# DLRM tower on one Trainium2 core: each 128-row gather is issued only when the one before it has landed

## The chip, the core and the metric

The kernel runs on one NeuronCore of one Trainium2 chip. Five engines work from queues of their own and meet through semaphores: TensorE (PE) multiplies, VectorE (DVE) and ScalarE (ACT) work element by element, GpSimd (POOL) here only issues gathers, and SyncE (SP) issues the plain transfers. All transfers share 16 DMA engines. The metric is device time in microseconds of one execution, lower being better; it is given as the median of several runs.

## What is computed

A batch of 2048 samples has 32 table ids each. Every id picks a row of 64 fp32 numbers from one of 32 tables, and all 496 pairs of these rows are combined through a 64 x 64 matrix of their own. The results, with 16 dense numbers per sample, go through three small layers. The reference, cut to what matters:

```python
def _L0_rec_ref(x, kernel):                       # x: [2048, 32, 64]
    row_idx, col_idx = np.triu_indices(nf, k=1)
    p = x[:, row_idx, :]
    q = x[:, col_idx, :]
    kp = jnp.einsum('bpe,fpe,bpf->bp', p, kernel, q)
    return kp
e = jnp.stack([tbl_0[ids[:, 0]], tbl_1[ids[:, 1]], ...], axis=1)
z = _L0_rec_ref(e, L0_rec_kernel)
h = jnp.concatenate([z, dense_ctx], axis=1)
h = jnp.maximum(h @ W_top1 + b_top1, 0.0)
h = jnp.maximum(h @ W_top2 + b_top2, 0.0)
y = h @ W_top3
```

## The kernel before

**Tiling.** A gather fetches one table's rows for 128 samples: 128 rows of 256 bytes, 32 KB, one row per partition. There are 16 sample tiles and 32 tables, so 512 gathers. The samples are cut into four chunks of 512 and worked on in five segments `g`: chunk 0 as two segments of two tiles, chunks 1 to 3 as one segment of four tiles each. Two tables make a pair `q` (16 pairs); a pair takes 4 gathers in the first two segments and 8 in the last three.

**POOL.** After it has made a small identity matrix, POOL has nothing in its queue but the 512 gathers (line 375 before, 383 after), in the order segment, pair, table of the pair, tile. Pairs 0 to 3 go to `kept_rows` (two copies, by chunk parity); pairs 4 to 15 go to `rows`, a ring of four pairs (`ROW_RING`). So the gathers of pair q wait, once per pair, until PE has turned pair q-4 (semaphore `unit_ready`), and the kept pairs of chunks 2 and 3 wait for the last product of the chunk two before. Apart from these waits POOL issues one gather behind the other and never asks whether one has landed. Each gather adds 16 to the semaphore `landed(g, q)` of its pair's buffer when it has landed; it is PE that waits for these, in `turn`.

**PE, DVE and ACT.** A list `ORDER`, written out by hand through `BURSTS`, sets one order of 566 units for all engines. A "turn" unit transposes the gathered rows of one or two pairs (line 433) and DVE copies them to `xt` (line 743). "duo" and "quad" units multiply transposed pairs with their matrices on PE (lines 475 to 491), and DVE multiplies the result with another pair (lines 712, 720). "batch" units do the same against the kept pairs (PE lines 497 and 499, DVE line 731), and ACT (or DVE for some) sums their products (line 637). PE then adds up the products over partitions (line 511) and computes the layers (lines 527, 530; the last chunk's in `last_tower`, lines 544 to 559). PE's results go through a ring of three PSUM buffers `y_ps`, ACT's sums through a ring of four. A turn of pair q comes at the place that `ORDER` gives it, and everything behind it on PE waits with it.

**SP.** At the start SP loads the ids, the pair matrices (7.75 MB) and the weights; later it copies small pieces between `xt` and `special`, and writes the outputs.

Of the kernel before, what the change touches and what calls it, by code (L numbers as in the profile page):

```python
# [17 lines left out]
SEGMENTS = ((0, 0, 2), (0, 2, 4), (1, 0, 4), (2, 0, 4), (3, 0, 4))  # L18
PAIRS = F // 2

KEPT = 4
ROW_RING = 4
# [21 lines left out]
def chunk(g):  # L44
    return SEGMENTS[g][0]


def tiles(g):

    return range(SEGMENTS[g][1], SEGMENTS[g][2])  # L50
# [10 lines left out]
def first_of(c):  # L61
    return min(g for g in range(len(SEGMENTS)) if chunk(g) == c)
# [17 lines left out]
def duo_order():  # L80

    duos = []
    for q in range(1, PAIRS):
# [5 lines left out]
        elif q == PAIRS - 1:  # L89
# [14 lines left out]
LAYERS = ([(1, n, kb) for n in range(4) for kb in range(4)] + [(2, n, kb) for n in range(2) for kb in range(4)]  # L104
          + [(3, 0, kb) for kb in range(2)])
GROUPS = 7
BANK_ENDS = [min(QUADS, Z_QUADS * (kb + 1)) - 1 for kb in range(Z_BANKS)]


# [70 lines left out]
TURN_OF = {(unit[1], q): g for g, unit in enumerate(UNIT) if unit[0] == "turn" for q in unit[2]}  # L180
# [44 lines left out]
def dlrm_tower(nc, ids, tables, pair_kernel, dense, w1, b1, w2, b2, w3, out):  # L225
    with ExitStack() as ctx:
# [3 lines left out]
        def sem(name):  # L230
            return ctx.enter_context(nc.semaphore(name))
# [41 lines left out]
        unit_ready = sem("unit_ready")  # L273
# [15 lines left out]
        def rows_of(g, q, t):  # L289
            if q < KEPT:  # L290
                return kept_rows[:, chunk(g) % 2, t, 2 * q:2 * q + 2]
            return rows[:, (q - KEPT) % ROW_RING, t]

        def lane(g):

            return int(SEGMENTS[g][1] > 0)

        def landed(g, q):
            return kept_landed[lane(g)][q] if q < KEPT else rows_landed[lane(g)][(q - KEPT) % ROW_RING]

        def landings(g, q):

            uses, own = (1, 1) if q < KEPT else ((PAIRS - KEPT) // ROW_RING, (q - KEPT) // ROW_RING + 1)
            before = sum(len(tiles(i)) for i in range(g) if lane(i) == lane(g))
            return 2 * 16 * (uses * before + own * len(tiles(g)))

        def z_of(c, kb):
            return z_sb[:, (c * Z_BANKS + kb) % Z_RING] if kb < Z_BANKS else z_turned[:]

# [37 lines left out]
        def group(c, layer, n):  # L347
            return c * GROUPS + {1: n, 2: 4 + n, 3: 6}[layer]

        block = ctx.enter_context(nc.Block())  # L350

        @block.gpsimd
        def _(pool):
            nc.gpsimd.memset(identity[:], 0.0).then_inc(identity_cleared, 1)
            pool.wait_ge(identity_cleared, 1)
            nc.gpsimd.affine_select(out=identity[:], in_=identity[:], compare_op=ALU.not_equal, fill=1.0, base=0,
                                    pattern=[[-1, P]], channel_multiplier=1).then_inc(identity_made, 1)
            for g in range(len(SEGMENTS)):
                c, before = chunk(g), first_of(chunk(g)) - 1
                if g == 0:  # L360
                    pool.wait_ge(ids_landed[0], 16)
                elif g == first_of(1):
                    pool.wait_ge(ids_landed[1], 16)
                for q in range(PAIRS):
                    if q < KEPT and c >= 2:
                        pool.wait_ge(unit_done, max(UNIT_OF[unit] for unit in BATCH if chunk(unit[1]) == c - 2) + 1)
                    elif q >= KEPT + ROW_RING:
                        pool.wait_ge(unit_ready, TURN_OF[g, q - ROW_RING] + 1)
                    elif q >= KEPT and c:
                        pool.wait_ge(unit_ready, TURN_OF[before, q - ROW_RING + PAIRS - KEPT] + 1)  # L370
                    for h in range(2):
                        j = 2 * q + h
                        for t in tiles(g):
                            n = c * TILES + t
                            pool.indirect_dma_start(rows_of(g, q, t)[:, h, :], None, tables[j],  # L375
                                                    bass.IndirectOffsetOnAxis(ap=idx[:, n, j:j + 1], axis=0)
                                                    ).then_inc(landed(g, q), 16)
# [50 lines left out]
        def _(pe):  # L428
# [74 lines left out]
            def add_up(g, quad):  # L503
# [5 lines left out]
                for m in range(4):  # L509
                    slot, place = product_of(g, 2 * quad + m // 2)  # L510
                    last = nc.tensor.matmul(sum_ps[32 * m:32 * m + 32, columns(g)], selector[:, 30 - 2 * s:62 - 2 * s],  # L511
                                            products[:, slot, m % 2, place],
                                            start=(s == 0 and not last_bank), stop=(quad in BANK_ENDS))
                last.then_inc(quad_summed, 1)
# [90 lines left out]
        def _(act):  # L605
# [3 lines left out]
            def copy_bank(g, kb):  # L609
                act.wait_ge(quad_summed, SUM_OF[g, BANK_ENDS[kb]] + 1)  # L610
                c = chunk(g)
                if c and kb == 1:
                    act.wait_ge(layer_ready, group(c - 1, 1, 3) + 1)
                copy(z_of(c, kb)[:, columns(g)], sum_ps[:, columns(g)]).then_inc(bank_kept, 1)
# [28 lines left out]
            for step in ORDER:  # L643
                kind = step[0]
                if kind == "sum" and step[2] in BANK_ENDS:
                    copy_bank(step[1], step[2] // Z_QUADS)
# [147 lines left out]
```

## Time and profile before

| | us |
|---|---|
| median of 3 runs | 1267.82 |
| lowest and highest run | 1261.34 to 1269.45 |
| span of the profiled execution | 1281.0 |
| of which PE busy / DVE busy / ACT busy | 845.6 / 656.8 / 685.0 |
| POOL busy (512 gathers and a few small instructions) | 484.9 |

The profiled execution is 13 us (1.0%) above the median. An engine is "busy" while it executes; a POOL row for a gather covers only the making of the transfer's descriptors, not the transfer. The transfer itself shows as packets on the DMA queue called software_dynamic: 16384 of them in all, so 32 for each gather: 16 of 2 KB with the rows and 16 of 4 bytes that raise the semaphore.

### The profile page before, as it was taken

To read this page: it belongs to the slowest core of one execution; us is meant where nothing else is said; L and a number is where in the kernel's file an instruction comes from. 1 tells how busy PE (TensorE), PEld (TensorE's weight loads), DVE (VectorE), ACT (ScalarE), POOL (GpSimd) and SP (SyncE) were. 2 spreads that over 40 slices of the span, in tenths; PEclk is the share of its full clock that TensorE was granted. 3 is DMA by queue.
4 is the path that set the end of the run, shared out by engine and by line. 5 is a ranking of instruction groups with operands and counts; after the bars stand their busy time and mean duration, and the time that the engine had idled before them with its cause. 6 is when DMAs were issued, how large, how long until landed. Compare 5 with 4: busy or idle time off the path is not lost.

```text
span 1281.0 us, 16495 instructions
## 1 busy us (share of the span) xinstructions
PE 845.6 (66%) x4672; PEld 330.6 (26%) x4672; DVE 656.8 (51%) x601; ACT 685.0 (53%) x5196; POOL 484.9 (38%) x518
## 2 busy tenths in 40 slices
PE   0570596603589658526899566028898856889999
PEld 0230253301344212102233122002233312223333
DVE  0350495401467445215689355016697545768881
ACT  0281295713255643106698525226696645779991
POOL 7557204575302454762400643755402244220000
PEclk9785697856789778757889777558899888889999
DMA  9111001111001110110101110210000101010000
GB/s 335 30 38 26 10 10 26 28 27 28 15 13 25 34 19 17 41 25 9 33 2 20 24 32 14 43 19 17 18 17 9 27 17 34 9 26 2 1 18 1
DMA packets 34644, 36.40 MB, mean 28 GB/s; under 512 B 18676, under 2 KB 20980, under 8 KB 34424
## 3 DMA queue, kind: packets, MB, share of 16 engines
q0 software_dynamic: 16384, 16.81, 7.1%
q1 hardware_dynamic: 18168, 18.53, 5.1%
q8 instruction: 37, 0.61, 0.2%
q14 instruction: 55, 0.45, 0.1%
HBM read 26.91 MB, written 0.01 MB: 21 GB/s over the span
## 4 chain that ended last, share of the span: by engine, by line
PE 45%; another core or an unknown queue 29%; issue 12%; DVE 11%; POOL 1%; DMA 1%; ACT 0%; DVEq 0%
PE y_ps L475 12%; PE y_ps L497 10%; PE sum_ps L511 8%; DVE batch_products L731 4%; DVE products L720 4%; PE layer_ps L527 4%; PE y_ps L490 3%; PE layer_ps L530 2%; DVE products L712 2%; PE y_ps L433 2%; POOL kept_rows L375 1%; PE y_ps L478 1%; PE y_ps L544 1%; PE y_ps L491 1%
## 5 line engine op out<-in xcount | busy, mean ns | idle before, releaser
L637 ACT ACTIVATE batch_products<-batch_products 128x64 f32<-128x64 f32 x2576 | 618.5, 243 | 298.8 <-issue 170.5
L375 POOL DMA_INDIRECT rows<-tbl_dram,idx x384 | 363.1, 945 | 613.3 <-PE y_ps L433 490.1
L637 ACT ACTIVATION_READ_ACCUMULATOR batch_products<-batch_products 128x1 f32 x2576 | 488.4, 190 | 123.2 <-issue 122.0
L720 DVE TENSOR_TENSOR products<-y_ps,xt 128x1024 f32<-128x1024 f32 (+1 forms) x224 | 258.5, 1200 | 260.8 <-remote 194.2
L475 PE MATMUL y_ps<-xt,kernel_sb 64*128 64x512 f32 (+1 forms) x448 | 233.3, 649 | 137.5 <-issue 78.5
L731 DVE TENSOR_TENSOR batch_products<-y_ps,kept_rows 128x1024 f32<-128x1024 f32 x192 | 225.5, 1217 | 92.7 <-remote 56.1
L497 PE MATMUL y_ps<-kernel_sb,xt 64*128 64x512 f32 x384 | 214.0, 683 | 71.7 <-DVE products L720 24.6
L476 PE MATMUL y_ps<-xt,kernel_sb 64*128 64x512 f32 (+1 forms) x448 | 233.4, 649 | 0.0
L499 PE MATMUL y_ps<-kernel_sb,xt 64*128 64x512 f32 x384 | 213.8, 683 | 0.0
L511 PE MATMUL sum_ps<-products,selector 128*32 128x512 f32 (+1 forms) x1520 | 162.4, 543 | 26.3 <-issue 10.9
L712 DVE TENSOR_TENSOR products<-y_ps,xt 128x1024 f32<-128x1024 f32 x68 | 79.8, 1218 | 160.5 <-remote 95.2
L475 PEld LDWEIGHTS y_ps<-xt,kernel_sb 64*128 64x128 f32 x448 | 80.5, 197 | 279.4 <-issue 172.2
L490 PE MATMUL y_ps<-xt,kernel_sb 64*128 64x256 f32 x272 | 83.0, 447 | 84.9 <-issue 46.5
L375 POOL DMA_INDIRECT kept_rows<-tbl_dram,idx x128 | 121.2, 947 | 40.3 <-issue 38.7
L497 PEld LDWEIGHTS y_ps<-kernel_sb,xt 64*128 64x128 f32 x384 | 72.2, 210 | 168.7 <-issue 60.6
L491 PE MATMUL y_ps<-xt,kernel_sb 64*128 64x256 f32 x272 | 83.7, 449 | 9.8 <-issue 9.8
L490 PEld LDWEIGHTS y_ps<-xt,kernel_sb 64*128 64x128 f32 x272 | 56.2, 217 | 106.4 <-issue 54.4
L476 PEld LDWEIGHTS y_ps<-xt,kernel_sb 64*128 64x128 f32 x448 | 80.4, 197 | 0.0
L511 PEld LDWEIGHTS sum_ps<-products,selector 128*32 128x32 f32 x1520 | 42.3, 114 | 136.6 <-issue 71.4
L743 DVE COPY xt<-y_ps 128x512 f32<-128x512 f32 (+2 forms) x58 | 42.6, 738 | 65.3 <-PE y_ps L433 43.2
L499 PEld LDWEIGHTS y_ps<-kernel_sb,xt 64*128 64x128 f32 x384 | 72.2, 210 | 0.2
L491 PEld LDWEIGHTS y_ps<-xt,kernel_sb 64*128 64x128 f32 x272 | 56.5, 218 | 14.0 <-issue 13.6
(54 smaller groups left out, 415.2 us busy)
## 6 DMA issues: line engine op xcount, KB each, us to landing
kernel_sb<-pair_kernel_dram SPq DMA_DIRECT2D x15, 512.0 KB, 4.9
rows<-tbl_dram,idx POOLq DMA_INDIRECT x384
special<-xt SPq DMA_DIRECT2D x48, 128.0 KB
kept_rows<-tbl_dram,idx POOLq DMA_INDIRECT x128
special<-xt SPq DMA_DIRECT2D x32, 64.0 KB
w_sb<-w_dram SPq DMA_DIRECT2D x1, 1024.0 KB
w_sb<-w_dram SPq DMA_DIRECT2D x1, 512.0 KB
kernel_sb<-pair_kernel_dram SPq DMA_DIRECT2D x1, 256.0 KB, 2.7
```

The costliest lines, as they stand in the source:

```text
L375: pool.indirect_dma_start(rows_of(g, q, t)[:, h, :], None, tables[j], bass.IndirectOffsetOnAxis(ap=idx[:, n, j:j + 1], axis=0)).then_inc(l ...
L475: nc.tensor.matmul(y[:, 0, :], kernel_sb[low, d, :], x_of(g, q)[low, :], start=True, stop=True)
L476: last = nc.tensor.matmul(y[:, 1, :], kernel_sb[high, d, :], x_of(g, q)[high, :], start=True, stop=True)
L490: nc.tensor.matmul(y[:, 0, place], kernel_sb[low, d, :], x_of(g, q)[low, :], start=True, stop=True)
L491: last = nc.tensor.matmul(y[:, 1, place], kernel_sb[high, d, :], x_of(g, q)[high, :], start=True, stop=True)
L497: nc.tensor.matmul(y[:, 0, :], x[low, :], kernel_sb[low, d:d + KEPT, :].rearrange("p d f -> p (d f)"), start=True, stop=True)
L499: nc.tensor.matmul(y[:, 1, :], x[high, :], kernel_sb[high, d:d + KEPT, :].rearrange("p d f -> p (d f)"), start=True, stop=True).then_inc(u ...
L511: last = nc.tensor.matmul(sum_ps[32 * m:32 * m + 32, columns(g)], selector[:, 30 - 2 * s:62 - 2 * s], products[:, slot, m % 2, place], sta ...
L637: last = nc.scalar.activation(product, product, ACT.Copy, accum_out=batch_sums(unit)[:, column:column + 1])
L712: nc.vector.tensor_tensor(into.rearrange("p b (d n) -> p b d n", d=2), y[:].rearrange("p b (d n) -> p b d n", d=2), by, ALU.mult).then_inc ...
L720: nc.vector.tensor_tensor(into[:, :, 0:size], y[:, :, 0:size], by, ALU.mult).then_inc(unit_done, 1)
L731: nc.vector.tensor_tensor(into, y[:], by, ALU.mult).then_inc(unit_done, 1)
```

## The change

One wait is put in front of every gather but the first. `FLIGHT` lists the 512 gathers in the order of issue; before a gather is issued, POOL waits until the semaphore of the gather issued last has reached the count that it has when exactly that gather has landed (`landed_by`).

```diff
+FLIGHT = [(g, q, h, t) for g in range(len(SEGMENTS)) for q in range(PAIRS) for h in range(2) for t in tiles(g)]
...
+        def landed_by(g, q, h, t):
+
+            return landings(g, q) - 16 * ((1 - h) * len(tiles(g)) + tiles(g)[-1] - t)
...
-                c, before = chunk(g), first_of(chunk(g)) - 1
+                c, last = chunk(g), first_of(chunk(g)) - 1
...
-                        pool.wait_ge(unit_ready, TURN_OF[before, q - ROW_RING + PAIRS - KEPT] + 1)
+                        pool.wait_ge(unit_ready, TURN_OF[last, q - ROW_RING + PAIRS - KEPT] + 1)
                     for h in range(2):
                         j = 2 * q + h
                         for t in tiles(g):
                             n = c * TILES + t
+                            if FLIGHT.index((g, q, h, t)):
+                                before = FLIGHT[FLIGHT.index((g, q, h, t)) - 1]
+                                pool.wait_ge(landed(*before[:2]), landed_by(*before))
                             pool.indirect_dma_start(rows_of(g, q, t)[:, h, :], None, tables[j],
```

`FLIGHT` and `before` are evaluated when the program is built; on the chip only the waits are new. The renaming of `before` to `last` changes nothing. No instruction of another engine is added, removed or moved.

POOL's queue at the start of the first segment, before the change, with the semaphores that each gather waits for:

```order
L375 DMA kept_rows<-tbl_dram,idx 128x64 [waits ids_landed0]
L375 DMA kept_rows<-tbl_dram,idx 128x64 x15
L375 DMA rows<-tbl_dram,idx 128x64 x16
L375 DMA rows<-tbl_dram,idx 128x64 [waits unit_ready]
L375 DMA rows<-tbl_dram,idx 128x64 x3
```

The same place after the change, where `kept_landed` and `rows_landed` are the semaphores that the gathers themselves raise:

```order
L383 DMA kept_rows<-tbl_dram,idx 128x64 [waits ids_landed0]
L383 DMA kept_rows<-tbl_dram,idx 128x64 [waits kept_landed0_0] x4
L383 DMA kept_rows<-tbl_dram,idx 128x64 [waits kept_landed0_1] x4
L383 DMA kept_rows<-tbl_dram,idx 128x64 [waits kept_landed0_2] x4
L383 DMA kept_rows<-tbl_dram,idx 128x64 [waits kept_landed0_3] x3
L383 DMA rows<-tbl_dram,idx 128x64 [waits kept_landed0_3]
L383 DMA rows<-tbl_dram,idx 128x64 [waits rows_landed0_0] x4
L383 DMA rows<-tbl_dram,idx 128x64 [waits rows_landed0_1] x4
L383 DMA rows<-tbl_dram,idx 128x64 [waits rows_landed0_2] x4
L383 DMA rows<-tbl_dram,idx 128x64 [waits rows_landed0_3] x3
L383 DMA rows<-tbl_dram,idx 128x64 [waits rows_landed0_3,unit_ready]
```

Before, 31 gathers in a row stood behind the first with no wait at all. Now each one waits for its predecessor, and the waits for the ring stay where they were.

## Rows read from the trace of the kernel before

**Rows 1.** The page: busy time, tenths over 40 slices, shares of the chain.
```profile
PE 845.6 (66%) x4672; PEld 330.6 (26%) x4672; DVE 656.8 (51%) x601; ACT 685.0 (53%) x5196; POOL 484.9 (38%) x518
...
DVE  0350495401467445215689355016697545768881
...
POOL 7557204575302454762400643755402244220000
PEclk9785697856789778757889777558899888889999
...
PE 45%; another core or an unknown queue 29%; issue 12%; DVE 11%; POOL 1%; DMA 1%; ACT 0%; DVEq 0%
```
**Rows 2.** The chain that ended last, 85 to 300 us: start, us, what.
```profile
92.61 41.02 issue
...
246.39 39.95 another core or an unknown queue
```
**Rows 3.** Windows inside long rows of gathers: bounds, length, busy us (instructions) per engine.
```profile
core 0: us, PE busy (x) PEld busy (x) DVE busy (x) ACT busy (x) POOL busy (x), PEclk, DMA share, GB/s
92.60:133.60 41.00, 3.17 (x14) 1.15 (x10) 0.01 (x1) 8.86 (x46) 31.18 (x33) 0.57 0.15 27
247.00:292.00 45.00, 3.85 (x32) 2.35 (x28) 1.23 (x2) 10.80 (x56) 34.00 (x36) 0.56 0.15 27
800.00:854.00 54.00, 6.58 (x24) 2.02 (x20) 2.45 (x2) 11.11 (x53) 40.89 (x44) 0.55 0.18 36
```
**Rows 4.** Windows with (almost) no gather, same columns.
```profile
640.00:702.60 62.60, 59.25 (x328) 21.52 (x330) 55.38 (x49) 58.59 (x478) 0.03 (x1) 0.95 0.06 11
1139.50:1253.00 113.50, 111.40 (x558) 39.70 (x560) 95.39 (x85) 103.07 (x828) 0.00 (x0) 0.97 0.03 6
```
**Rows 5.** The first 5 us of a row of 40 gathers, same columns.
```profile
87.60:92.60 5.00, 5.00 (x46) 2.52 (x48) 5.00 (x5) 5.00 (x44) 3.78 (x5) 1.00 0.26 68
```
**Rows 6.** POOL's gathers by line: xcount, busy us, mean ns, idle before them.
```profile
L375 POOL DMA_INDIRECT rows<-tbl_dram,idx x384 | 363.1, 945 | 613.3 <-PE y_ps L433 490.1 <-issue 105.8 <-remote 15.8
L375 POOL DMA_INDIRECT kept_rows<-tbl_dram,idx x128 | 121.2, 947 | 40.3 <-issue 38.7 <-DMA idx<-ids_dram 1.6
```
**Rows 7.** Timeline around four gathers: start, us, engine, idle before and releaser.
```profile
3.02 1.10 POOL L375 DMA_INDIRECT kept_rows<-tbl_dram,idx  x1 [1.55 <-DMA idx<-ids_dram]
...
81.45 0.95 POOL L375 DMA_INDIRECT rows<-tbl_dram,idx  x1 [0.30 <-issue]
82.70 0.95 POOL L375 DMA_INDIRECT rows<-tbl_dram,idx  x1 [0.30 <-issue]
...
86.92 0.41 PE L433 MATMUL y_ps<-identity,rows 64*128 64x64 f32 x8
87.60 0.94 POOL L375 DMA_INDIRECT rows<-tbl_dram,idx  x1 [3.95 <-PE y_ps L433]
```
**Rows 8.** DMA packets from 82.69 us, first up to 84.79, then up to 84.85.
```profile
DMA packets 64, 0.07 MB, mean 35 GB/s; under 512 B 31, under 2 KB 31, under 8 KB 63
...
DMA packets 65, 0.07 MB, mean 34 GB/s; under 512 B 32, under 2 KB 32, under 8 KB 64
```
**Rows 9.** DMA packets from 0.70 us, first up to 2.39, then up to 2.45.
```profile
DMA packets 151, 0.08 MB, mean 49 GB/s; under 512 B 15, under 2 KB 143, under 8 KB 151
...
DMA packets 155, 0.09 MB, mean 50 GB/s; under 512 B 16, under 2 KB 144, under 8 KB 155
```
**Rows 10.** A gather's way under load (chain, 0 to 60 us); DMA queues, 0 to 33 us.
```profile
26.95 5.76 DMA rows<-tbl_dram,idx
...
q1 hardware_dynamic: 5397, 10.05, 86.8%
```
**Rows 11.** The last turns of the program on PE: start, us, engine line.
```profile
1155.55 0.46 PE L433 MATMUL y_ps<-identity,rows 64*128 64x64 f32 x8
...
1192.10 0.46 PE L433 MATMUL y_ps<-identity,rows 64*128 64x64 f32 x8
...
1221.16 0.46 PE L433 MATMUL y_ps<-identity,rows 64*128 64x64 f32 x8
```

## The prediction, made before the changed kernel was run

> **What bounds the kernel now.** I read the page first. No engine is busy for more than 66% of the 1281.0 us, and 41% of the chain that ended last is work of nobody: 29% "another core or an unknown queue" and 12% "issue" [rows 1]. The line of DVE over 40 slices is low where that of POOL is high, and the granted TensorE clock falls there too. Then I read the longest pieces of that chain: 41.02 us from 92.61 and 39.95 us from 246.39 [rows 2]. Windows laid over them show what they are. Each lies inside a long row of gathers issued back to back (40, 40 and 48 gathers around the three windows). In 41 us of the first, DVE does nothing, PE executes 14 matmuls and ACT 46 instructions, while POOL goes on with 33 gathers [rows 3]. In windows without gathers the same program keeps PE busy for 98% of 113.5 us and 95% of 62.6 us, DVE for 84% and 88% [rows 4]. The first five microseconds of a row of gathers are not slow: PE, DVE and ACT are busy all the time in 87.60:92.60 [rows 5], and the standstill begins right behind them. So the kernel has two kinds of time: without gathers, where PE and DVE are nearly full, and long rows of gathers, where everybody but POOL all but stands still. POOL itself is no bound: of its idle time before the `rows` gathers 490.1 us of 613.3 is a wait for PE's turns [rows 6].
>
> How much is lost: DVE's 656.8 us busy at 84 to 88% would take 750 to 780 us. The other 500 of 1281.0 are start-up (33 us) and time beside gathers. The change could give much of that back, since it spaces the gathers. What it costs is POOL's own pace.
>
> **The change part by part.** Nothing is removed or moved. 511 waits are added on POOL, and behind a waiting gather stand only further gathers; PE's turns wait for those, and DVE and ACT for PE. The ring waits stay. What counts is the period, from the start of one gather to the start of the next.
>
> Before, it is 1.25 us: 82.70 less 81.45 [rows 7], that is 0.95 execution and 0.30 to the next. After, it is the way of one gather to its semaphore plus POOL's reaction.
>
> - The way: between 82.69 and 87.60 fall the packets of two gathers, that of 82.70 and the one before it, with 32 packets under 512 B. Up to 84.79, 31 of them have run, up to 84.85 all 32 [rows 8]. So the last four-byte packet runs 2.1 to 2.15 us after the start: 2.12.
> - The reaction: the trace has no gather that waits for another. The nearest row is POOL's wait for the ids: their 16th small packet has run by 2.42 (between 2.39 and 2.45) [rows 9], and POOL starts at 3.02 [rows 7], 0.60 later. The lower bound is the reaction to an engine's semaphore: PE's turn ends at 87.33 and POOL starts at 87.60 [rows 7], 0.27. I take 0.58, near the first, since that also is a semaphore raised by DMA packets.
>
> The period is then 2.70 us, with 2.39 and 2.75 as bounds. At the start it is longer: while SP's loads keep the DMA engines 87% busy, a gather took 5.76 us to land [rows 10]; with 0.27 that makes 6.0. From 3.0 to 33 us that is 5 gathers. The other 507 at 2.70 take 1369 us, so the last gather lands at about 1402 us. That alone is more than the span of 1281.0. In the old kernel POOL needed 512 x 1.25 = 640 us and waited for the rest.
>
> Does POOL also wait for the ring in between? A pair of 8 gathers takes 21.6 us, and POOL runs up to four pairs ahead. Without standstills PE needs about 780 us for what amounts to 64 such pairs, 12 us each. So PE waits for POOL and the ring is empty; I put POOL's ring waits at 0. The gain from no standstills is hidden in these waits of PE: it makes PE faster between turns, where it then waits anyway.
>
> The tail: PE turned pair 13 of the last segment at 1155.55, pair 14 at 1192.10, pair 15 at 1221.16, and ended at 1281.0 [rows 11]. From turn 13 to the end is 125.5 us, at nearly full speed with no gathers beside it [rows 4]. The steps between, 36.6 and 29.1, are both longer than 21.6, so once pair 13 has landed PE is behind and works through. Pair 13 lands 16 gathers before the last: 1402 - 16 x 2.70 = 1359. The end is 1359 + 125.5 = 1484 us. In a formula: 33 + (507 - 16) x period + 125.5. The measured median lies 13 us below the profiled span, so 1471; I say 1470, 16% slower.
>
> Two rules of the Trainium skill bear on this. DMA: Bandwidth & Descriptors, section "Anatomy of one DMA — SWDGE (gpsimd) path", gives a gather of this kind about 2.0 us plus bytes over 436 GB/s, an estimate of 2.08 us for 32 KB; the trace's 2.12 to the last packet agrees. If that figure held all the way to the semaphore, with 0.27 for the reaction, the period would be 2.35 and the end 33 + 491 x 2.35 + 125.5 = 1312, so 1299; that falls into the second rival below. Trainium Architecture — The Big Picture, section "What this means for kernel authors", says that the engines are independent processors and that one does not block another unless a semaphore stands between them. By that rule gathers could not hold up DVE, and spacing them would give nothing back. What slows DVE in a row of gathers would then be something else and could remain, which is the first rival's time. The trace speaks against the rule here: in 41 us with 33 gathers DVE did 0.01 us of work [rows 3].
>
> **The rivals.**
> - *The standstill stays.* Each gather costs the other engines a fixed time, however far apart the gathers are. In the three windows DVE is busy for 3.7 of 140 us, 3% [rows 3] against 84%, so it loses 1.2 of each 1.25 us; with the free start of a row [rows 5] I take 1.1. At a period of 2.70 they would then run at 1 - 1.1/2.70 = 60% of full speed, and 780 us of work would take 1300, close to POOL's 1369, so PE would fall behind where `ORDER` has much work between turns. The two steps of the tail, 65.6 us, would take up to 109, and PE would come to turn 13 some 30 us late: 1484 + 43 + 30 = 1557, so about 1545. For it: only that the mechanism isn't known. Against it: five gathers in [rows 5] cost nothing at all, so what fails fails through a build-up, and at 2.70 us there is more than twice the time to drain it.
> - *The reaction is short.* With 0.27 the period is 2.39, the end 33 + 491 x 2.39 + 125.5 = 1332, so 1319. For it: the PE row. Against it: the ids row.
> - *Not slower.* The standstills go, and a gather that runs alone lands sooner than one with a neighbour. It decides where 33 + 491 x period + 125.5 is 1281, at a period of 2.28 us. The packets alone take 2.12, so only 0.16 would be left for the semaphore and POOL, less than the smallest reaction seen, 0.27. And packets of neighbours don't overlap now: 81.45 and 82.70 are 1.25 apart. To be faster by 1% the period would have to be 2.25.
> - *PE at the lower clock.* PE will wait often, and in windows where it waits much the granted clock is 0.55 to 0.57 of full speed [rows 3], which is mostly the 1.2 GHz level, against 0.95 and 0.97 where it works [rows 4]. Between turns there is slack for this; in the tail it may cost 10 to 40 us. That gives up to 1510.
>
> **How the numbers follow.** The forecast (period 2.6 to 2.75, other engines nearly free, 1430 to 1500) gets 0.65; the lower clock or some leftover standstill with 1500 to 1560 gets 0.2; a short reaction with 1310 to 1430 gets 0.11; not slower gets 0.04. The range is 1395 to 1550: it leaves out a little of both ends. A measurement of this kernel can tell about 1% from no change. Slower by over 1%: 0.96; within 1%: 0.02; faster: 0.02.
>
> **What would show it.** POOL's gathers should start 2.7 us apart almost without exception from 33 us on, with "DMA" as releaser, and its wait for PE's turns (490.1 us now) should be close to nothing. The last gather should start near 1400 us. PE should wait for DMA in front of nearly every turn, and the pieces of 40 us of "issue" and "unknown queue" should be gone. If DVE's busy share between turns stays low while PE has landed rows to turn, the first rival holds. The prediction is wrong if gathers come less than 2.4 us apart, or if POOL waits for turns again.

## The result and the profile after

| | kernel before | changed kernel |
|---|---|---|
| median, us | 1267.3 (4 runs, 1261.34 to 1269.45) | 1536.18 (4 runs, 1531.42 to 1538.41) |
| profiled execution: time / span | span 1281.0 | 1536.28 / 1534.5 |
| mean granted TensorE clock, share of full speed | 0.813 | 0.779 |

The change makes the kernel 21% slower: the ratio is 1.212, with a 95% interval of 1.208 to 1.216. 1470 was forecast, with a range of 1395 to 1550. The time lies in the range, 66 us above the forecast.

The page of the changed kernel, first the busy times, then the tenths over 40 slices, last the shares of the chain that ended last (these answer to [rows 1]):

```profile
PE 838.8 (55%) x4672; PEld 342.6 (22%) x4672; DVE 659.8 (43%) x601; ACT 646.7 (42%) x5196; POOL 483.5 (32%) x518
...
DVE  0033740435514324326474203543572435664882
...
PEclk9986975768757767779697556876896777897999
...
DMA 74%; PE 15%; issue 10%; DVE 1%; DVEq 0%; ACT 0%; POOLq 0%
```

The work is the same, but the chain is another. "Another core or an unknown queue" was 29% of it and is gone. 74% of the chain is now "DMA": one gather behind the other on its way to its semaphore.

POOL's gathers by line, with the idle time before them and its releasers (answers to [rows 6]), and then PE's two longest waits (total us, times, longest):

```profile
L383 POOL DMA_INDIRECT rows<-tbl_dram,idx x384 | 362.0, 943 | 716.5 <-DMA rows<-tbl_dram,idx 658.9 <-PE y_ps L441 40.0 <-DMA kept_rows<-tbl_dram,idx 5.6
L383 POOL DMA_INDIRECT kept_rows<-tbl_dram,idx x128 | 120.8, 944 | 248.7 <-DMA kept_rows<-tbl_dram,idx 228.0 <-DMA rows<-tbl_dram,idx 8.5 <-issue 5.9
```
```profile
PE y_ps L441 <- DMA rows<-tbl_dram,idx: 500.3, 50, 22.8
PE y_ps L441 <- DMA kept_rows<-tbl_dram,idx: 187.0, 15, 26.7
```

POOL now waits for landings, 658.9 + 5.6 + 228.0 + 8.5 = 901 us in all, where it had waited 490.1 us for PE's turns. PE waits for rows 65 times, 687 us in all.

The timeline of POOL at three places: start, us, then in brackets the idle time before it and what ended it.

```profile
31.17 0.94 POOL L383 DMA_INDIRECT kept_rows<-tbl_dram,idx  x1 [3.41 <-DMA kept_rows<-tbl_dram,idx]
...
101.36 0.94 POOL L383 DMA_INDIRECT rows<-tbl_dram,idx  x1 [1.74 <-DMA rows<-tbl_dram,idx]
104.54 0.94 POOL L383 DMA_INDIRECT rows<-tbl_dram,idx  x1 [2.24 <-PE y_ps L441]
107.21 0.94 POOL L383 DMA_INDIRECT rows<-tbl_dram,idx  x1 [1.73 <-DMA rows<-tbl_dram,idx]
...
1445.69 0.94 POOL L383 DMA_INDIRECT rows<-tbl_dram,idx  x1 [1.75 <-DMA rows<-tbl_dram,idx]
1448.44 0.94 POOL L383 DMA_INDIRECT rows<-tbl_dram,idx  x1 [1.81 <-DMA rows<-tbl_dram,idx]
```

The step from 104.54 to 107.21 is 2.67 us and that from 1445.69 to 1448.44 is 2.75; over the whole trace the median step is 2.70. But the step from 101.36 to 104.54 is 3.18 us. The gather at 104.54 is the first of a pair, so it has the wait for the ring in front of its landing wait. The last gather starts at 1448.4.

Two windows of the changed kernel near its end, one with gathers and one without (columns as in [rows 3]):

```profile
core 0: us, PE busy (x) PEld busy (x) DVE busy (x) ACT busy (x) POOL busy (x), PEclk, DMA share, GB/s
...
1410.00:1448.00 38.00, 38.00 (x176) 13.62 (x174) 29.85 (x27) 34.70 (x281) 12.87 (x14) 0.98 0.07 13
1450.00:1505.00 55.00, 54.94 (x292) 19.66 (x286) 46.19 (x41) 51.25 (x414) 0.00 (x0) 1.00 0.05 11
```

With 14 gathers in 38 us, PE is busy all of the time and DVE for 79% of it, against 84% in the window with none. At this pace gathers hardly disturb anybody. In the rows of the kernel before DVE was busy for 0.01 us of 41 [rows 3].

The last turns on PE (start, us, what; they answer to [rows 11]):

```profile
1406.37 0.69 PE L441 MATMUL y_ps<-identity,rows 64*128 64x64 f32 x8 [10.67 <-DMA rows<-tbl_dram,idx]
...
1445.54 0.46 PE L441 MATMUL y_ps<-identity,rows 64*128 64x64 f32 x8
...
1474.61 0.46 PE L441 MATMUL y_ps<-identity,rows 64*128 64x64 f32 x8
```

Pair 13 is the last for which PE waits, 10.67 us. Behind it PE works through: 39.2 us to the next turn, 29.1 to the one after, 59.9 to the end.

### The profile page after: what moved, and what is told of

It reads as the page before. It is cut to its first block, busy times and chain, and to the rows that moved or that the text cites. A ratio compares the mean times of both kernels' runs of the same rounds, so it can differ in the third digit from the quotient of the medians.

```text
span 1534.5 us, 16556 instructions
## 1 busy us (share of the span) xinstructions
PE 838.8 (55%) x4672; PEld 342.6 (22%) x4672; DVE 659.8 (43%) x601; ACT 646.7 (42%) x5196; POOL 483.5 (32%) x518
## 4 chain that ended last, share of the span: by engine, by line
DMA 74%; PE 15%; issue 10%; DVE 1%; DVEq 0%; ACT 0%; POOLq 0%
DMA rows<-tbl_dram,idx 55%; DMA kept_rows<-tbl_dram,idx 19%; PE y_ps L505 4%; PE y_ps L483 4%; PE sum_ps L519 3%; PE y_ps L441 1%; PE layer_ps L535 1%; PE layer_ps L538 1%; PE y_ps L552 1%; PE y_ps L498 1%; PE y_ps L561 0%; DVE products L728 0%; PE y_ps L556 0%; DMA idx<-ids_dram 0%; PE y_ps L486 0%
## 5 line engine op out<-in xcount | busy, mean ns | idle before, releaser
L383 POOL DMA_INDIRECT rows<-tbl_dram,idx x384 | 362.0, 943 | 716.5 <-DMA rows<-tbl_dram,idx 658.9
L441 PE MATMUL y_ps<-identity,rows 64*128 64x64 f32 x384 | 33.0, 300 | 500.6 <-DMA rows<-tbl_dram,idx 500.3
L505 PE MATMUL y_ps<-kernel_sb,xt 64*128 64x512 f32 x384 | 245.0, 780 | 1.7 <-DVE xt L751 1.5
L507 PE MATMUL y_ps<-kernel_sb,xt 64*128 64x512 f32 x384 | 244.8, 780 | 0.0
L483 PE MATMUL y_ps<-xt,kernel_sb 64*128 64x512 f32 (+1 forms) x448 | 208.9, 601 | 0.3 <-DVE products L728 0.3
L484 PE MATMUL y_ps<-xt,kernel_sb 64*128 64x512 f32 (+1 forms) x448 | 208.9, 601 | 0.0
L383 POOL DMA_INDIRECT kept_rows<-tbl_dram,idx x128 | 120.8, 944 | 248.7 <-DMA kept_rows<-tbl_dram,idx 228.0
L519 PE MATMUL sum_ps<-products,selector 128*32 128x512 f32 (+1 forms) x1520 | 172.2, 571 | 3.1 <-DVE products L720 1.4
L441 PEld LDWEIGHTS y_ps<-identity,rows 64*128 64x128 f32 x384 | 23.9, 189 | 533.9 <-issue 288.2
L441 PE MATMUL y_ps<-identity,kept_rows 64*128 64x64 f32 x128 | 11.0, 302 | 187.4 <-DMA kept_rows<-tbl_dram,idx 187.0
L505 PEld LDWEIGHTS y_ps<-kernel_sb,xt 64*128 64x128 f32 x384 | 88.3, 249 | 104.5 <-issue 61.2
L483 PEld LDWEIGHTS y_ps<-xt,kernel_sb 64*128 64x128 f32 x448 | 78.8, 188 | 134.0 <-issue 81.0
L507 PEld LDWEIGHTS y_ps<-kernel_sb,xt 64*128 64x128 f32 x384 | 88.3, 249 | 0.0
L484 PEld LDWEIGHTS y_ps<-xt,kernel_sb 64*128 64x128 f32 x448 | 78.8, 188 | 0.0
L498 PE MATMUL y_ps<-xt,kernel_sb 64*128 64x256 f32 x272 | 71.2, 410 | 0.3 <-DVE products L720 0.3
```

The costliest lines, as they stand in the source:

```text
L441: return nc.tensor.transpose(into, rows_of_tile[part, :], identity[part, part])
L483: nc.tensor.matmul(y[:, 0, :], kernel_sb[low, d, :], x_of(g, q)[low, :], start=True, stop=True)
L484: last = nc.tensor.matmul(y[:, 1, :], kernel_sb[high, d, :], x_of(g, q)[high, :], start=True, stop=True)
L498: nc.tensor.matmul(y[:, 0, place], kernel_sb[low, d, :], x_of(g, q)[low, :], start=True, stop=True)
L505: nc.tensor.matmul(y[:, 0, :], x[low, :], kernel_sb[low, d:d + KEPT, :].rearrange("p d f -> p (d f)"), start=True, stop=True)
L507: nc.tensor.matmul(y[:, 1, :], x[high, :], kernel_sb[high, d:d + KEPT, :].rearrange("p d f -> p (d f)"), start=True, stop=True).then_inc(u ...
```

## The experiments

Two questions were open. Where do the 66 us over the forecast come from? And what is the standstill beside rows of gathers, which the change removes at so high a price? The runs were made in four groups, each with the kernel before beside it, and the groups differ in a way that nothing in the profile of before had announced:

| runs | kernel before beside them, us |
|---|---|
| chip A: every 2nd, every 4th, every 8th, extra wait | 1266.95 |
| chip B: every 6th, spacer, few sums, plain transfers | 794.48 (13 runs, 794.44 to 795.12) |
| chip C: changed kernel again, spacer again | 794.43 (7 runs) |
| chip D: ring wait last, a repeat of the kernel before | 1287.12 (13 runs, 1279.88 to 1291.69) |

The same program takes 1267 to 1287 us on two chips and 794 us on two others. Which chip the main result came from isn't on record; its two times, 1267.3 and 1536.18 us, are those of chip A (1266.95, and 1536.48 with the extra wait), and it is counted with A below. Each ratio is against the kernel before on the same chip.

### Fewer landing waits: every 2nd, 4th, 8th gather (chip A)

In the changed kernel only every 2nd gather waits for the one ahead of it; in two more kernels the 2 is a 4 and an 8. Between waiting gathers POOL issues back to back.

```diff
-                            if FLIGHT.index((g, q, h, t)):
+                            if FLIGHT.index((g, q, h, t)) and FLIGHT.index((g, q, h, t)) % 2 == 0:
```

Expected of every 2nd:

> POOL waits only ahead of every second gather, until the gather issued last has landed; the other is issued straight behind its neighbour. Two gathers then take 1.25 + 2.8 us, a mean pace of 2.0 us. Theory A (the standstill of the other engines builds up over a row of back-to-back gathers and drains in a gap; spaced gathers cost the others nothing): POOL's pace sets the end, 33 + 491 x 2.0 + 125.5 = 1140 us, and no piece of standstill is left. Rival B (each gather costs the others a fixed 0.9 us wherever it stands: before, 1281 less 33 less 780 is 468 us over 512 gathers): the others need 33 + 780 + 468 = 1281 whatever POOL does, so about 1280 us.

Expected of every 4th:

> The wait stands ahead of every fourth gather: three at 1.25 us and one at 2.8, a mean pace of 1.64 us. Theory A with a build-up that takes more than four gathers and drains in one gap: PE becomes the bound in the heavy stretches, POOL in the others, 33 + 491 x 1.64 + 125.5 = 965 us, up to 1050. If the gap of 1.5 us behind four gathers doesn't drain what they build up, standstills come back and the time lies above that of the kernel with every second. Rival B: about 1280 us.

Expected of every 8th:

> The wait stands ahead of every eighth gather: a mean pace of 1.44 us. Before, the others worked for about five gathers of a long row and then stood. Theory A: standstills return in the last gathers of each eight and in long rows carry over, so 1100 to 1250 us, slower than every fourth; if the gap drains everything, 870 to 1000. Rival B: about 1280 us.

Measured: every 2nd 1167.56 us (ratio 0.921, 0.917 to 0.925), every 4th 990.98 us (0.782, 0.779 to 0.785), every 8th 1106.45 us (0.874, 0.870 to 0.878). All three are faster than the kernel before on this chip, and the one in the middle is the fastest. The chain's shares, every 2nd first, then every 4th and every 8th:

```profile
DMA 44%; PE 26%; POOL 16%; issue 12%; DVE 2%; DVEq 0%; ACT 0%; POOLq 0%
```
```profile
PE 48%; POOL 21%; DMA 19%; issue 10%; DVE 2%; DVEq 0%; ACT 0%; POOLq 0%
```
```profile
PE 49%; another core or an unknown queue 14%; issue 13%; DVE 12%; ACT 8%; POOL 2%; DMA 2%; DVEq 0%
```

At every 2nd the chain is still the gathers' own way (DMA and POOL, 60%). At every 4th PE is the largest part and nothing of the standstill is left: DVE has two waits of 1.9 us in all that the trace puts down to an unknown queue, where in the kernel before there are 50 of 374.5 us. At every 8th the "unknown queue" is back with 14%. A window of every 4th in which most of the time goes to gathers, then one of every 8th:

```profile
core 0: us, PE busy (x) PEld busy (x) DVE busy (x) ACT busy (x) POOL busy (x), PEclk, DMA share, GB/s
242.00:283.00 41.00, 26.48 (x252) 14.88 (x252) 26.33 (x24) 20.32 (x168) 23.73 (x26) 0.91 0.13 27
```
```profile
core 0: us, PE busy (x) PEld busy (x) DVE busy (x) ACT busy (x) POOL busy (x), PEclk, DMA share, GB/s
246.30:261.60 15.30, 5.61 (x28) 2.96 (x24) 0.00 (x0) 7.05 (x51) 9.45 (x11) 0.68 0.13 24
```

With 26 gathers in 41 us DVE is busy for 26.33 us; with 11 in 15.3 us it does nothing. The timeline of every 8th shows how the standstill comes and goes, DVE's rows first, then POOL's:

```profile
244.98 1.23 DVE L739 TENSOR_TENSOR batch_products<-y_ps,kept_rows 128x1024 f32<-128x1024 f32 x1 [0.48 <-issue]
261.70 1.23 DVE L720 TENSOR_TENSOR products<-y_ps,xt 128x1024 f32<-128x1024 f32 x1 [15.50 <-remote]
```
```profile
240.00 0.95 POOL L383 DMA_INDIRECT kept_rows<-tbl_dram,idx  x1 [0.48 <-issue]
...
247.51 0.94 POOL L383 DMA_INDIRECT kept_rows<-tbl_dram,idx  x1 [0.30 <-issue]
250.17 0.94 POOL L383 DMA_INDIRECT kept_rows<-tbl_dram,idx  x1 [1.72 <-DMA kept_rows<-tbl_dram,idx]
...
261.56 0.95 POOL L383 DMA_INDIRECT kept_rows<-tbl_dram,idx  x1 [1.69 <-DMA kept_rows<-tbl_dram,idx]
```

DVE stops at 246.2, when six gathers of a group have been issued. A pause of POOL of 1.72 us at 250.17 does not set it free; it starts again only at 261.70, right behind the next one. So the price of the standstill is not so much per gather. It needs a build-up of more than four gathers, as [rows 5] had suggested, and once there it can outlast one pause. The build-up view forecast every 4th and every 8th rightly (965 to 1050, and 1100 to 1250) and every 2nd 28 us too low, with a mean pace of 2.0 us where 2.09 was measured; "each gather costs a fixed time" (1280 for every 2nd) was wrong by 112 us.

### An extra wait behind the landing wait (chip A)

Is the missing time a price per semaphore wait? POOL gets one more wait in front of every gather but the first, for a semaphore that was raised long ago.

```diff
                                 pool.wait_ge(landed(*before[:2]), landed_by(*before))
+                                pool.wait_ge(identity_cleared, 1)
```

> The changed kernel with one more wait ahead of each gather but the first, on a semaphore that has been up since the start. In the changed kernel POOL starts 0.58 us after a gather's last packet where it has one wait, and 1.05 us where the ring's wait stands there too, in 60 of 512 places. Theory C (a second wait instruction costs POOL 0.47 us though it is met): 511 x 0.47 = 240 us more, about 1775 us. Rival (the 0.47 us is a property of these places, such as a turn that was only just done): about 1535 us.

Measured: 1536.48 us (2 runs), beside the changed kernel's 1536.18. A met wait that stands behind the landing wait costs nothing; 511 of them change the time by 0.3 us. The price per wait is ruled out for this place. Ahead of the landing wait it is another matter, as the next run shows.

### The ring wait behind the landing wait (chip D)

In 60 places a gather of the changed kernel waits first for the ring (or for the last product of the chunk two before) and then for the landing. Here the two waits change places.

```diff
                     for h in range(2):
                         j = 2 * q + h
                         for t in tiles(g):
                             n = c * TILES + t
                             if FLIGHT.index((g, q, h, t)):
                                 before = FLIGHT[FLIGHT.index((g, q, h, t)) - 1]
                                 pool.wait_ge(landed(*before[:2]), landed_by(*before))
+                            if (h, t) == (0, tiles(g)[0]) and q < KEPT and c >= 2:
+                                pool.wait_ge(unit_done, max(UNIT_OF[unit] for unit in BATCH if chunk(unit[1]) == c - 2) + 1)
+                            elif (h, t) == (0, tiles(g)[0]) and q >= KEPT + ROW_RING:
+                                pool.wait_ge(unit_ready, TURN_OF[g, q - ROW_RING] + 1)
...
```

> The changed kernel with the two waits of a pair's first gather in the other order: first the landing of the gather before, then the ring's turn of PE (or the last product), in 60 places. In the changed kernel these gathers start 1.05 us after the last packet of the one before, all others 0.58; a met extra wait behind the landing wait cost nothing. Theory D (a landing wait costs 0.47 us more when another wait stands ahead of it): these too start after 0.58, the last gather starts 28 us earlier, the end is 1536 less 28, about 1508 us. Rival (the ring's wait itself is slow, in either order): about 1535 us.

Measured: 1513.76 us (1506.95 to 1518.03), ratio 1.174 (1.168 to 1.180) to the 1287.12 of chip D. The changed kernel itself did not run on chip D, so the comparison of times is across chips; the rows carry the argument. This is the gather that started 3.18 us behind its predecessor in the changed kernel:

```profile
101.73 0.94 POOL L383 DMA_INDIRECT rows<-tbl_dram,idx  x1 [1.81 <-DMA rows<-tbl_dram,idx]
104.42 0.94 POOL L383 DMA_INDIRECT rows<-tbl_dram,idx  x1 [1.74 <-DMA rows<-tbl_dram,idx]
...
1429.28 0.94 POOL L383 DMA_INDIRECT rows<-tbl_dram,idx  x1 [1.82 <-DMA rows<-tbl_dram,idx]
```

It now takes 2.69 us. Over all 60 such gathers the time from the last packet of the one ahead to the start is 0.56 us at the median, where it was 1.05 in the changed kernel and 0.58 for all other gathers. So 60 x 0.47 = 28 us of the changed kernel's time was the order of two waits. The last gather starts at 1429.3, only 19 us sooner, and the time is 1514 where 1508 was expected: in this run the ways were longer (2.141 us at the mean against 2.125, 8 us over 506 steps), as were the other landing waits (0.626 against 0.619, 3 us). One more place agrees. The first gather of chunk 1 has the wait for the second half of the ids, long met, ahead of its landing wait in both kernels, and it starts 1.09 and 1.04 us after the last packet. It isn't a wait for PE: in the changed kernel PE was itself waiting for rows. The releaser that the profile names for these gathers, PE's line 441 (40.0 us in 18 waits), is only the semaphore that stood first.

### Does the changed kernel know of the standstill? (chip C)

No edit; the changed kernel runs where the kernel before takes 794 us.

> The changed kernel as it is, once more. In the last four runs the kernel before took 794.5 us beside them, not 1267: no stretch in which all engines but GpSimd stand. Those four kernels therefore say what gathers cost without a standstill. Where the kernel before takes 1267 us here, this one should take 1536 again. Where it takes 794, theory P (the end is GpSimd's chain of gathers, and standstills play no part in it) gives 33 + 491 x 2.70 + 125.5 = 1484 us, up to 1536 if the late reactions of 1.05 us are there as well; the ratio to before would be 1.87 to 1.93 instead of 1.21. The rival (the changed kernel too lost time to standstills, 50 us or more) gives below 1440.

Measured: 1534.81 us (1532.74 to 1538.73), ratio 1.933 (1.930 to 1.937), with a span of 1531.4, the last gather at 1447.0 and a clock of 0.782. On chip A it took 1536.18. The changed kernel has the same time in both places; all the difference lies in the kernel before. The change costs 269 us in one and 740 in the other, and what could be worked out is the absolute time.

### Every 6th gather (chip B)

The 4 above is a 6.

```diff
-                            if FLIGHT.index((g, q, h, t)):
+                            if FLIGHT.index((g, q, h, t)) and FLIGHT.index((g, q, h, t)) % 6 == 0:
```

> The wait ahead of every sixth gather; mean pace 5 x 1.25 + 2.8, over 6, is 1.51 us. Measured so far: every gather 1536, every second 1168, every fourth 991, every eighth 1106 us, never 1267. Theory A: about five gathers are free and then the others stand, so six are near the turning point: 985 to 1050 us, above every fourth by what one or two gathers of standstill in each six cost (85 groups of about 1 us: 1030). If the pace alone counted (no standstill at six) it would be 960 to 980.

Measured: 912.12 us, ratio 1.148 (1.146 to 1.150) to the 794.48 there. It lies below both expectations, also below the 960 to 980 given for pace alone; that figure was too high by the prediction's own formula, which gives 900 us for a pace of 1.51 and 915 for the measured 1.54. Whether six gathers start a standstill can't be told from this run, since the kernel before shows no lost time on this chip. What it gives is one more point on how the end follows POOL's pace, taken up in the next section.

### A fixed pace without any landing wait (chips B and C)

The kernel before gets one small memset on POOL between gathers, and the next gather but one waits for it, so that gathers start farther apart, whether they have landed or not. It was to tell a standstill by rate from one by gathers in flight.

```diff
+                            i = FLIGHT.index((g, q, h, t))
+                            if i > 1:
+                                pool.wait_ge(paced, i - 1)
+                            if i:
+                                nc.gpsimd.memset(pace[:], 0.0).then_inc(paced, 1)
                             pool.indirect_dma_start(rows_of(g, q, t)[:, h, :], None, tables[j],
```

> The kernel before with no wait for a landing, but with one small memset on GpSimd between each gather and the next (its result is used by nobody), which should space the gathers evenly by 1.5 to 1.9 us. A gather takes 2.1 us to its last packet, so the next is always begun before the last has landed: the pipe never runs empty. Theory R (what counts is the rate of gathers; at this pace nothing builds up): no standstill, and the end near 33 + 491 x pace + 125.5, so 935 at 1.65, 1010 at 1.8. Theory L (what counts is that gathers land before the next is issued, an empty pipe now and then): long standstills remain, 1150 us or more.

> The kernel with a small memset between gathers and no wait for a landing, once more; it spaced the gathers by 1.39 us and took 849 us where the kernel before took 794. Where the kernel before takes 794 here: 849 again. Where it takes 1267, theory L (only an empty pipe now and then ends a build-up) gives a time near 1267 or above, 1150 to 1350; theory R (the rate counts) gives clearly less, 900 to 1100, since the rate is 11% lower at 1.39 us.

Measured: 848.86 us on chip B (ratio 1.068, 1.066 to 1.070) and 848.02 on chip C (1.068, 1.066 to 1.069). The gathers start 1.39 us apart, less than the 1.5 to 1.9 expected, and the chain's shares on chip B are:

```profile
POOL 55%; PE 36%; issue 8%; DMA 1%; DVEq 0%; POOLq 0%; DVE 0%; ACT 0%
```

So 0.14 us more per gather makes POOL the bound of a kernel in which, at 1.25, PE was nearly full (93% in the kernel with few sums below, where the last gather starts at 657.4, 56 us sooner, and the end comes 55 us sooner). Rate against in flight stays undecided: neither chip has a standstill to remove. A third kernel was meant for chip D, with three memsets per gather, but the one that ran held the tile and the semaphore for them and none of the memsets:

```diff
+        pace = sb("pace", [P, 192])
...
+        paced = sem("paced")
```

> No wait for a landing; three small memsets, each waiting for the one before, stand between gathers, in place of one. With one the pace was 1.39 us. Three should make it 2.1 to 2.4. Theory P (the end follows GpSimd's pace, whatever makes it): 3 + 495 x pace + 2.4 + 125.5, the start-up now without landing waits, so 1170 at 2.1 and 1320 at 2.4. Rival (waits for landing cost the other engines something beyond the pace): below this formula by more than 20 us. Where the kernel before takes 1267 us and not 794, theory L of the spacer kernel would put this one above the formula, with standstills; theory R on it.

Measured: 1285.57 us against 1287.12, ratio 0.999 (0.996 to 1.001). That is the kernel before once more, and nothing about pace follows from it. Its chain has the same kind of piece at the same place as [rows 2]:

```profile
92.54 46.55 another core or an unknown queue
```

### Three quarters of ACT's sums left out (chip B)

In the kernel before, ACT sums the products of every fourth column only; the rest of that result is zero. The question was whether the many small instructions of ACT make the standstill.

```diff
+                if column % 4 < 3:
+                    return
...
-            nc.vector.memset(z_batch[:, :, 0, :], 0.0).then_inc(z_cleared, 1)
+            nc.vector.memset(z_batch[:], 0.0).then_inc(z_cleared, 1)
```

> The kernel before (no waits for landing) in which ScalarE sums only every fourth of its columns, so the output lacks these sums; ScalarE issues 3864 instructions fewer of 16495. ScalarE was not the bound. Theory S (gathers and the instructions of all engines draw on one shared thing, so fewer instructions of ScalarE leave more for PE and DVE): the standstills begin later and the time falls well below 1267, to 1100 to 1200. Rival (a row of gathers stops each engine by itself): 1240 to 1270 us.

Measured: 794.38 us against 794.48, ratio 1.000 (0.999 to 1.001). ACT's busy time falls from 685.0 to 195.0 us and the time doesn't move, so ACT is far from the bound; on the standstill the run is silent. Its profile shows long rows of gathers at full pace on a chip without standstills. The page's busy times, and two windows:

```profile
PE 739.7 (93%) x4672; PEld 302.6 (38%) x4672; DVE 650.1 (82%) x601; ACT 195.0 (25%) x1332; POOL 484.1 (61%) x518
```
```profile
core 0: us, PE busy (x) PEld busy (x) DVE busy (x) ACT busy (x) POOL busy (x), PEclk, DMA share, GB/s
200.00:241.00 41.00, 37.05 (x283) 17.84 (x280) 33.34 (x30) 7.89 (x55) 30.94 (x34) 1.00 0.22 41
300.00:341.00 41.00, 41.00 (x226) 14.73 (x224) 36.96 (x35) 14.10 (x102) 30.94 (x34) 1.00 0.19 40
```

34 gathers in 41 us, as dense as in [rows 3] (33 in 41), and DVE is busy for 33 and 37 us, PE for 37 and 41. This kernel has fewer instructions of ACT than the kernel before, but on this chip their times are equal.

### Plain transfers in place of gathers (chip B)

The kernel before, with each gather replaced by a plain transfer from POOL's queue of the same shape, which always fetches a table's first 128 rows, so the results are of the wrong rows.

```diff
-                            pool.indirect_dma_start(rows_of(g, q, t)[:, h, :], None, tables[j],
-                                                    bass.IndirectOffsetOnAxis(ap=idx[:, n, j:j + 1], axis=0)
-                                                    ).then_inc(landed(g, q), 16)
+                            pool.dma_start(rows_of(g, q, t)[:, h, :], tables[j][0:P, :]).then_inc(landed(g, q), 16)
```

> The kernel before with each indirect gather replaced by a plain transfer of the first 128 rows of the same table, issued from GpSimd as before (so the rows are the wrong ones): same bytes, same destinations, same queue, same semaphores, no waits for landing. If the standstill comes from GpSimd-made transfers as such, long rows of them stop the engines again and the time is near 1267 where the pace is the same (1.0 to 1.3 us each). If it comes from the indirect form, there are no standstills and the time is 850 to 950 us.

Measured: 783.16 us (2 runs), ratio 0.986 (0.984 to 0.988). POOL's busy time is 270.3 us in place of 484.9, so 0.53 us for a transfer in place of 0.95. Being rid of the indirect form is worth 11 us on a chip without standstills. Whether plain transfers would cause one elsewhere is open.

## Why the prediction was right, and where its 66 us went

**How the end follows POOL.** In the runs in which the gathers' own pace sets the time, the end is the start of the last gather plus a tail, as the forecast had it.

| | mean pace, us | last gather starts | span | tail |
|---|---|---|---|---|
| changed kernel | 2.80 | 1448.4 | 1534.5 | 86 |
| ring wait last | 2.76 | 1429.3 | 1516.2 | 87 |
| every 2nd | 2.09 | 1071.3 | 1168.1 | 97 |
| every 4th | 1.71 | 878.6 | 993.9 | 115 |
| every 6th | 1.54 | 791.4 | 911.8 | 120 |
| spacer, chip B | 1.39 | 713.8 | 847.8 | 134 |

The forecast's tail was 1484 less the start of the last gather, about 1399: 85 us. Measured 86. It grows at faster paces, presumably because PE then has more left to do when the last gather lands. Every 8th is not in the table: there POOL waits for PE's turns again (227.5 us; mean pace 1.87, last gather at 960.1, tail 143), and the pace doesn't set the end.

Step by step:

- *The period, 2.70 us (2.12 way + 0.58 reaction).* Right as the median of the steps, to the hundredth. The ids row, not the PE row, was the one to go by. Single landing waits took 0.58 us at the median from the last packet to the start.
- *507 gathers at this period.* **The step that failed.** A typical step was taken for the mean. The mean from 31.17 to 1448.44 is 2.80 us (506 steps); 0.10 x 506 is 51 us, and the last gather starts 49 us later than forecast. 28 us of it are the 60 gathers that stand behind two waits (0.47 each), shown by the exchange of the waits. The rest, about 20 us, are single landing waits of more than 0.58 (their mean is 0.62, which makes 18 us over 446) and ways of more than 2.12 (mean 2.125, some 3 us); why these vary is open.
- *POOL's ring waits put at 0.* In the sense meant, right: PE was ahead, and no ring was ever full. But the wait instruction itself wasn't free where it stood, and the trace books 40.0 us under PE's name, most of which is the gather's own way running at the same time. The forecast priced the event and not the place of the wait.
- *The start-up, 5 gathers by 33 us.* Right: the gather behind the first five starts at 31.17. But its steps were 6.9, 5.5, 5.5, 5.8 and 4.3 us where 6.0 was taken for each, so the agreement of the sum is in part luck.
- *The tail from turn 13.* 128.1 us against 125.5, its steps 39.2 and 29.1 against 36.6 and 29.1. Pair 13 was turned at 1406.4, 47 us after the 1359 forecast; this is the mean period again.
- *Minus 13 us for the median.* Wrong. The 13 us between the median and the span of before belonged to one execution of the kernel before and not to the profile as such. It may have been how long its standstills lasted, or another chip (on chip D its spans are 1278 to 1290 us); the record doesn't tell. The changed kernel's profiled execution took 1536.28 us, 1.8 above its span and level with its median. This step cost 13 + 2 us.

Summed: 47 (pair 13 late) + 3 (tail) + 13 + 2 = 65, and the miss is 66 us.

**The rivals.** *The standstill stays* named a time, 1545, that lies nearer to the result than the forecast, but its mechanism is refuted: with 14 gathers in 38 us PE is full, DVE is busy for 79%, and the two steps of the tail take 68.3 us together, where this rival had up to 109. *The short reaction* (2.39) and *not slower* (2.28; its equation gives 2.29) fall with the period. *PE at the lower clock*: in the window 1410 to 1448 the granted clock is 0.98, mostly the 2.4 GHz level, and 1.00 behind it, as PE waits for nothing there. In the slack it was low: the clock of 0.779 over the whole span shows it. It cost at most the 2.6 us by which the tail is longer.

The Trainium skill, DMA: Bandwidth & Descriptors, section "Anatomy of one DMA — SWDGE (gpsimd) path", gives about 2.0 us plus bytes over 436 GB/s, an estimate of 2.08 us here. By itself it is close to the 2.12 us to the last packet, but a kernel that chains gathers pays 2.70 per gather, and the forecast was right not to take the page's figure as the whole of it.

**The sign.** Slower needed only a period above 2.29 us, and with the shortest reaction in the rows it is 2.39: the chain of gathers and the tail together then outlast the kernel before. The picture of the kernel before that went with it, 500 us lost in standstills and start-up of which the change could give much back, fits chips A and D: the same kernel takes 473 and 493 us less on B. On chips B and C there is nothing to give back, and on C, where it was run, the change costs 93%. So the ratio forecast, 16% slower, holds only where the kernel before takes 1267 us; the absolute time doesn't depend on that.

The kernel that waits ahead of every 4th gather is 22% faster than the kernel before on chip A. It wasn't run on B or C; on B even every 6th is 15% slower than the kernel before. No version that was run is the best on both kinds of chip.

## What to carry to other kernels

A chain of waiting transfers is priced by the mean of issue to issue, so look for the links that carry a second wait: the landing wait goes first and the wait that is already met goes behind it. Where a burst of gathers starves the other engines, break the burst every few gathers rather than at each one: here one landing wait in four cost POOL 0.46 us per gather over back-to-back issue and left no standstill in the trace. Before a kernel is tuned against a stall that no semaphore explains, run it on another chip: here the kernel with all landing waits took 1536 us on one and 1535 on another, and what it was compared with differed by 60%.

## What the runs showed of the hardware

**The standstill came on two chips of four.** The same kernel takes 1266.95 and 1287.12 us on two chips and 794.48 and 794.43 us on two others, steady to 0.1% on the latter. The four groups of runs were made within half an hour in the order A, B, C, D, so slow, fast, fast, slow. Each chip was visited once: that the chip itself decides, and not something else that was so on it at that time, is likely but not shown, and what differs no run tells. The granted clock of the kernel before was 0.81 to 0.82 on A and D and 0.996 to 1.0 on B and C; inside the standstills, where PE all but stops, it was 0.55 to 0.57 [rows 3]. The Trainium skill's rule in Trainium Architecture — The Big Picture, section "What this means for kernel authors", that one engine doesn't block another without a semaphore, agrees with chip B (34 gathers in 41 us beside 33 us of DVE's work, in the kernel with few sums) and not with the profile of the kernel before (33 gathers beside 0.01 us, [rows 3]).

**What is known of it.** It begins some five or six gathers into a row at 1.25 us; groups of four never started it (every 4th), groups of eight did (every 8th), and it can outlast a single pause of 1.7 us. It isn't a full stop. ACT goes on with its sums through the first long row of the kernel before, and toward its end it starts exactly one instruction every 1.40 us, with no semaphore to wait for:

```profile
121.00 0.26 ACT L637 ACTIVATE batch_products<-batch_products 128x64 f32<-128x64 f32 x1 [1.21 <-issue]
122.39 0.20 ACT L637 ACTIVATION_READ_ACCUMULATOR batch_products<-batch_products 128x1 f32 x1 [1.14 <-issue]
```

Just ahead of the standstill it executed 44 in 5 us [rows 5]. Each still executes in 0.20 to 0.26 us. So for ACT it is the start of every single instruction that comes late, and the step of 1.40 us is not the gathers' 1.25. Late loading of instructions doesn't end it: from 87.8 to 145.4 us not one packet ran on the two instruction queues, and the standstill from 92.6 to 133.6 begins and ends in between. Whether it comes from the rate of issue or the number of gathers in flight, and whether the indirect form or ACT's small instructions have a part in it, stays open: the runs meant to tell fell on chips without it, or lacked the memsets.

**The order of waits has a price.** On POOL a wait already met costs 0.47 us ahead of a landing wait (1.05 against 0.58 us from the last packet to the start, 60 places) and nothing behind it (511 places, 0.3 us in all), as the exchange of the two waits showed (0.56 us). Why is open.
